# A two-stage FFN kernel: the second stage begins with the batches that the first one finished last

## The chip, the cores and the metric

One core of one Trainium2 chip runs the kernel. The metric is the device time of one execution in microseconds (us); the kernel before took 832.73 us (median of 3 runs, 832.57 to 832.79).

## The reference, cut to what is computed

```python
# x: (32, 128, 2048) f32; one session id, channel count and length for each of the 32 batches
xm  = x * channel_mask
h   = gelu(einsum('bct,bch->bht', xm, W_sess[ids]) + b_sess[ids][:, :, None])   # 128 -> 256
o   = (einsum('bht,hs->bst', h, W2) + b2) * time_mask                           # 256 -> 128
w_q = fp8_e4m3(clip(weight * w_scale))     # w_scale = 448 / max|weight|, weight is 2048 x 2048
x_q = fp8_e5m2(clip(o * x_scale))          # x_scale = 57344 / max|o| over ALL batches
out = x + einsum('bsk,nk->bsn', x_q, w_q) / x_scale / w_scale + bias
```

The scale of `o` needs the maximum over all 32 batches. So the second product can't begin before the first stage is through.

## The kernel before, in words

**Stage one** works in units `u` of 1024 columns, two for each of 32 batches, so u = 0 to 63. Per unit TensorE (PE) multiplies x by the session weight (12 matmuls at L980; x is split into a high and a low part), ScalarE (ACT) applies the gelu, and PE multiplies by W2. The first half of h is always split into a high and a low part (`project0`, 6 matmuls, L995). The second half (`project1`) is either split too, for the units in `SPLIT_H1` (6 matmuls, L1007; ACT writes one more copy at L621 and GpSimd (POOL) subtracts at L541), or is multiplied unsplit in fp32 (L1011; the profile counts 4 matmuls). VectorE (DVE) masks the output (`mask_o`, L765), scans it for its maximum (`scan_o`, L770) and makes the low part of h (`split_h_rest`, L755). SyncE (SP) stores `o` of each batch to `masked_out` in HBM (`store_o`).

**The FFN weight** is scanned for its maximum in 24 parts, one per unit. Then it is rounded to e4m3 in 43 chunks of 768 columns (the last has 512): ACT scales chunk i (`scale_chunk`, L633, which waits until chunk i-2 is rounded), DVE makes its rounding factor (`exponents` L779, `round_at` L784) and POOL adds and subtracts it (`round_chunk`, L535 and L537). `QUANT = SCANS + 2 = 26` says when that begins: POOL rounds chunk i in unit i + QUANT + 1. `EARLY_CHUNKS = 64 - 3 - QUANT = 35` chunks are rounded in stage one, and the 8 "late" ones (35 to 42) after it.

**The seam.** After the last unit DVE reduces the maximum (L844, L848), PE broadcasts it (L1052), DVE makes the scale (L850, L852, L854) and quantizes the first batch of stage two in 5 cuts (L861). PE turns each cut (L1065), ACT writes it back as fp8 (L702), and the products begin (L1071). In between PE runs a few matmuls whose result isn't read (L1047, 8 and then 4).

**Stage two** multiplies the 32 quantized batches by the rounded weight: for each batch 4 products (`n`) of 16 matmuls over 512 output columns, into 4 PSUM banks in turn. The first 16 products are written out as the list `FIRST`: y = 0 to 11 are n = 0, 1, 2 of batches 0 to 3, and y = 12 to 15 are n = 3 of the four. The first three products run side by side. The last quarter of the weight, chunks 32 to 42, is read from y = 12 on only. DVE takes each product out of its bank (`evacuate`, L881, or L901 for n = 3), adding `x + bias`. Product y waits until product y - 4 is out of the bank. Evacuation of n = 0 to 2 waits until POOL has added the bias to that batch's x (`add_bias`, L569, counted by `xb_ready`), and for n = 3 it waits for the small adds of L589 (`x3_ready`).

Each engine works strictly in the order of its program. Behind the seam:

- POOL: bias to x of batch 0 (ahead of the seam), chunks 35, 36, bias of batch 1, chunks 37 to 40, bias of batch 2 (`x2_more[0]`), chunks 41, 42, bias of batch 3 (`x2_more[1]`), four small adds (L589), and then one bias add per batch.
- DVE: 5 cuts, factor of chunk 35, quantization of batch 1, chunks 36 to 38; then, product by product, the evacuation, with the quantization of batches 2, 3 and 4 ahead of y = 2, 5, 10 (`QUANT_AT`) and the factor of a chunk behind y = 4, 5, 6, 7 (`CHUNK_BEHIND`).
- SP: the loads of `o` and x, the transposing DMAs (`turn`, `turn_more`) that lay a quantized batch out for PE, and the stores.

`o` of batches 0 and 1 is read back into `o_in` from unit 40 on, `o` of 2 and 3 after the seam; x of the first batches is read again from HBM.

```python
                dve.wait_ge(y_psum, y + 1 + ONE)          # DVE, product y of batch b
                if n < NC - 1:
                    dve.wait_ge(xb_ready, b + 1)
                    ...
                    evacuate(...)
                pe.wait_ge(y_ready, y + 1)                # PE, ahead of product y (starts at 4)
```

Of the kernel before, what the change touches and what calls it, by code (L numbers as in the profile page):

```python
# [6 lines left out]
def adaln_ffn(nc, x, ids, lens, counts, w_sess, b_sess, w2, b2, weight, bias, out, masked_out, split_w):  # L7
# [33 lines left out]

    SPLIT_H1 = [u for u in range(2, 27)]

# [6 lines left out]
    CHUNKS = -(-WCOLS // CHUNK)  # L50
    QUANT = SCANS + 2

# [12 lines left out]

    QUAD = 4
    FIRST = [(b, n) for b in range(QUAD) for n in range(NC - 1)] + [(b, NC - 1) for b in range(QUAD)]

# [3 lines left out]

    CHUNK_BEHIND = range(4, 12)
    TAIL = [slice(BANK * (NC - 1), BANK * NC - BANK // 2), slice(BANK * NC - BANK // 2, BANK * NC)]
# [8 lines left out]
    with ExitStack() as ctx:  # L83
# [86 lines left out]

        xs = x_sb[:, 1, :]
        q8 = xs[:, 0:T // 2].bitcast(fp8).rearrange("p (r t) -> p r t", r=2)
# [11 lines left out]

        x3 = sb_at("x3", [P, QUAD, BANK], fp32, xh_at)
        x2 = (x_sb[:, 0, :], h1[:, :, :].rearrange("p a n -> p (a n)"))
        x2_more = (sb_at("x2_more0", [P, T], fp32, hh_at)[:, :], sb_at("x2_more1", [P, T], fp32, hl_at)[:, :])
# [122 lines left out]
        def _(sp):  # L310
# [56 lines left out]
            for u in range(UNITS):  # L367
# [37 lines left out]
                if 0 <= i < CHUNKS:  # L405
                    if i >= 3:
                        sp.wait_ge(w_scaled, i - 2)
                    load_chunk(i)
                if u % UPB == 0 and b > 0:
                    sp.wait_ge(o_masked, u)  # L410
                    store_o(b - 1)
                if u == UNITS - 4:

                    sp.wait_ge(xl_ready, UNITS - 2)
                    load_x_again(0, 0, FRONT)
                if u == UNITS // 2:
                    sp.dma_start(bias_sb[:, :], bias.partition_broadcast(P)).then_inc(bias_loaded, 16)
                if u in (UNITS // 2 + 8, UNITS // 2 + 12):
# [24 lines left out]
            turn(1)  # L443
            for r in range(2):
                sp.wait_ge(o_stored[r], 2 * 16)
                load_o(2 + r, r)
            for r in range(2):
                sp.dma_start(x2_more[r][:, FRONT], x[2 + r, :, FRONT]).then_inc(x2_more_loaded[r], 16)
            for b in range(2):

                sp.wait_ge(q_ready, b + 2 + CUTS)
                sp.sem_inc(transpose_turn, 1)
                turn_more(b)
                if b == 1:
                    sp.wait_ge(o_stored[0], 3 * 16)
                    load_o(4, 0)
                    sp.dma_start(x3[:, :, :], x[0:QUAD, :, FRONT.stop:F].rearrange("b c t -> c b t"))\
                      .then_inc(x3_loaded, 16)
                sp.wait_ge(y_ready, (b + 1) * (NC - 1) + FREE4)
                store_y(b, b, FRONT)  # L460
            load_x_again(4, 0)
            sp.wait_ge(o_stored[1], 3 * 16)
            load_o(5, 1)
            load_x_again(5, 1)
            for b in range(2, QUAD):
                sp.wait_ge(y_ready, (b + 1) * (NC - 1) + FREE4)
                store_y(b, b % 2, FRONT)

# [5 lines left out]
            for b in range(QUAD):  # L474
                sp.wait_ge(y_ready, QUAD * (NC - 1) + b + 1 + FREE4)
                sp.dma_start(out[b, :, FRONT.stop:F], x3[:, b, :]).then_inc(y3_stored, 16)

            def step2(i, last):
                for r in range(2):
                    b = i * 2 + r  # L480
                    if not last:
                        sp.wait_ge(q_ready, b + CUTS)
                        load_o(b + 2, r)
                    if not (last and r == 1):
                        sp.wait_ge(y_psum, b * NC + ONE)
                        sp.sem_inc(load_turn, 1)
                        sp.wait_ge(q_ready, b + 1 + CUTS)
                        sp.sem_inc(transpose_turn, 1)
                        turn(1 - r)
                    if last and r == 1:  # L490
                        for n in range(NC - 1):
                            cols = slice(n * BANK, (n + 1) * BANK)
                            sp.wait_ge(y_ready, b * NC + n + 1 + FREE4)
                            sp.dma_start(out[b, :, cols], y_sb[:, r, cols]).then_inc(y_chunk_stored[n], 16)
                        for h, cols in enumerate(TAIL):
                            sp.wait_ge(y_ready, B * NC + h + FREE4)
                            sp.dma_start(out[b, :, cols], y_sb[:, r, cols]).then_inc(y_chunk_stored[NC - 1 + h], 16)
                        continue
                    sp.wait_ge(y_ready, (b + 1) * NC + FREE4)
                    store_y(b, r)  # L500
                    if not last:
                        load_x_again(b + 2, r)


            for r in range(2):
                sp.wait_ge(o_stored[r], 16 * STEPS)
            with sp.Fori(QUAD // 2, STEPS - 1) as i:
# [9 lines left out]
        def _(pool):  # L517
# [54 lines left out]
            pool.wait_ge(bias_loaded, 16)  # L572
            pool.wait_ge(x2_loaded[0], 16)
            add_bias(x2[0], FRONT)
            for i in late[0:2]:
                round_chunk(i)
            pool.wait_ge(x2_loaded[1], 16)
            add_bias(x2[1], FRONT)
            for i in late[2:6]:
                round_chunk(i)  # L580
            pool.wait_ge(x2_more_loaded[0], 16)
            add_bias(x2_more[0], FRONT)
            for i in late[6:]:
                round_chunk(i)
            pool.wait_ge(x2_more_loaded[1], 16)
            add_bias(x2_more[1], FRONT)
            pool.wait_ge(x3_loaded, 16)
            for b in range(QUAD):
                pool.tensor_tensor(x3[:, b, :], x3[:, b, :], bias_sb[:, FRONT.stop:F], ALU.add).then_inc(x3_ready, 1)  # L589
            with pool.Fori(QUAD // 2, STEPS) as i:  # L590
                for r in range(2):

                    pool.wait_ge(x2_loaded[r], i * 16)
                    add_bias(x2[r])

        @block.scalar
        def _(act):
# [77 lines left out]
            for u in range(UNITS):  # L675
# [39 lines left out]
        def _(dve):  # L715
# [94 lines left out]
            for u in range(UNITS):  # L810
                if u == SCANS + 2:
                    weight_scale()
                if u >= 1:
# [3 lines left out]
                    if u == SCANS + 1:  # L817
                        dve.wait_ge(w_scanned, SCANS)
                        dve.wait_ge(floor_ready, 2)
                        dve.tensor_reduce(w_pmax, w_max[:, :], AX.X, ALU.max).then_inc(w_pmax_ready, 1)  # L820
                    scan_o(u - 1, 0, slice(0, UNIT))
                if 0 <= u - QUANT - 1 < EARLY_CHUNKS + 1:
                    exponents(u - QUANT - 1)
                if 0 <= u - QUANT - 1 < EARLY_CHUNKS:
                    round_at(u - QUANT - 1)
                if u + 1 < UNITS:
                    split_h_rest(u + 1)
                if u == 0:
                    dve.tensor_copy(w2h1[:, :], w2_sb[:, 1, :]).then_inc(w2_split, 1)
# [319 lines left out]
```

## Time and profile before

| | before |
|---|---|
| median of 3 runs | 832.73 us |
| the profiled execution's own time | 833.1 us |
| its span, first to last instruction | 831.3 us |
| PE busy | 825.8 us (99%) |
| POOL busy | 511.8 us (62%) |
| DVE busy | 479.5 us (58%) |
| ACT busy | 345.9 us (42%) |
| PE's share of the chain that ended last | 99% |
| HBM read / written | 143.04 / 69.21 MB |

The span is what lies between the first and the last instruction; 1.8 us of the execution's time lie around it. PE is busy nearly all the time and is nearly all of the chain that ends last. So what counts is how many matmuls there are, and where PE stands still.

### The profile page before, as it was taken

To read this page: it belongs to the slowest core of one execution; us is meant where nothing else is said; L and a number is where in the kernel's file an instruction comes from. 1 tells how busy PE (TensorE), PEld (TensorE's weight loads), DVE (VectorE), ACT (ScalarE), POOL (GpSimd) and SP (SyncE) were. 2 spreads that over 40 slices of the span, in tenths; PEclk is the share of its full clock that TensorE was granted. 3 is DMA by queue.
4 is the path that set the end of the run, shared out by engine and by line. 5 is a ranking of instruction groups with operands and counts; after the bars stand their busy time and mean duration, and the time that the engine had idled before them with its cause. 6 is when DMAs were issued, how large, how long until landed. Compare 5 with 4: busy or idle time off the path is not lost.

```text
span 831.3 us, 10181 instructions
## 1 busy us (share of the span) xinstructions
PE 825.8 (99%) x3568; PEld 479.9 (58%) x3568; DVE 479.5 (58%) x499; ACT 345.9 (42%) x372; POOL 511.8 (62%) x238
## 2 busy tenths in 40 slices
PE   9999999999999999999999999999999999999998
PEld 5777777776767676765444444444444444444444
DVE  6989889788888888888553232323232323232322
ACT  7999999988888888973100000000000000000000
POOL 2899999899999999995983242424242423232322
PEclk9999999999999999999999999999999999999999
DMA  7988999877777877657974868686868686868682
GB/s 258 322 321 321 367 339 353 301 285 296 284 289 303 305 267 301 253 187 246 298 295 119 282 214 282 210 285 212 280 213 280 214 283 214 279 213 282 215 248 107
DMA packets 75008, 220.77 MB, mean 266 GB/s; under 512 B 37594, under 2 KB 40930, under 8 KB 55778
## 3 DMA queue, kind: packets, MB, share of 16 engines
q1 hardware_dynamic: 74080, 219.30, 74.5%
q10 hardware_dynamic: 898, 1.09, 0.4%
q8 instruction: 16, 0.26, 0.1%
q14 instruction: 14, 0.11, 0.0%
HBM read 143.04 MB, written 69.21 MB: 255 GB/s over the span
## 4 chain that ended last, share of the span: by engine, by line
PE 99%; issue 0%; POOL 0%; DVE 0%; ACT 0%; POOLq 0%
PE ps_h L1071 53%; PE ps_h L980 22%; PE ps_o L995 11%; PE ps_o L1011 8%; PE ps_o L1007 4%; PE ps_o L934 1%; PE ps_h L1047 0%; PE ps_o L1071 0%; PE ps_o L980 0%; PE ps_o L1065 0%; POOL time L518 0%; PE ps_o L940 0%; PE ps_h L1052 0%; DVE o_and_max L881 0%; ACT x_sb L702 0%
## 5 line engine op out<-in xcount | busy, mean ns | idle before, releaser
L1071 PE MATMUL ps_h<-wqT,x_sb 128*128 128x512 bf16 x1920 | 413.7, 378 | 0.2 <-ACT x_sb L702 0.2
L1071 PEld LDWEIGHTS ps_h<-wqT,x_sb 128*128 128x128 fp8e5 x1920 | 187.7, 98 | 224.4 <-ACT x_sb L702 0.3
L528 POOL TENSOR_TENSOR xl<-x_sb,xh 128x1024 fp32r<-128x1024 f32 x62 | 149.5, 2411 | 16.3 <-ACT xh L607 16.3
L980 PE MATMUL ps_h<-xh,whl 128*128 128x512 f32 x508 | 150.3, 417 | 0.4
L569 POOL TENSOR_TENSOR x_sb<-x_sb,bias_sb 128x2048 f32<-128x2048 f32 (+1 forms) x15 | 66.7, 4447 | 131.7 <-DMA x_sb<-in_x 131.7
L569 POOL TENSOR_TENSOR h<-h,bias_sb 128x2048 f32<-128x2048 f32 (+1 forms) x15 | 66.7, 4443 | 122.7 <-DMA h<-in_x 122.7
L881 DVE SCALAR_TENSOR_TENSOR o_and_max<-ps_h,scales,h 128x512 f32<-128x512 f32 (+1 forms) x59 | 44.0, 746 | 136.2 <-PE ps_h L1071 136.2
L881 DVE SCALAR_TENSOR_TENSOR o_and_max<-ps_h,scales,x_sb 128x512 f32<-128x512 f32 x59 | 44.2, 750 | 133.4 <-PE ps_h L1071 133.4
L980 PEld LDWEIGHTS ps_h<-xh,whl 128*128 128x128 f32 x508 | 94.2, 188 | 42.0 <-issue 21.7
L765 DVE SCALAR_TENSOR_TENSOR o_and_max<-ps_o,b_sb,steps 128x1024 f32<-128x1024 f32 (+1 forms) x65 | 82.2, 1264 | 29.0 <-PE ps_o L1011 27.1
L755 DVE TENSOR_TENSOR hl<-ps_h,hh 128x1024 fp32r<-128x1024 f32 x63 | 76.8, 1219 | 13.4 <-ACT ps_h L614 13.3
L535 POOL TENSOR_TENSOR ws<-ws,wc 128x768 f32<-128x768 f32 (+1 forms) x43 | 72.2, 1679 | 18.2 <-DVE wc L784 16.7
L613 ACT ACTIVATE hh<-ps_h,hbias 128x1024 fp32r<-128x1024 f32 x63 | 70.3, 1115 | 26.7 <-PE ps_h L980 26.7
L980 PE MATMUL ps_h<-xl,whl 128*128 128x512 f32 x254 | 79.1, 392 | 0.0
L770 DVE TENSOR_REDUCE o_max<-o_and_max 128x1 f32<-128x1024 f32 x64 | 77.6, 1212 | 2.2
L537 POOL TENSOR_TENSOR wqT<-ws,wc 128x768 bf16<-128x768 f32 (+1 forms) x43 | 71.8, 1669 | 3.4
L1011 PE MATMUL ps_o<-h,w_sb 128*128 128x512 f32 x156 | 73.4, 592 | 0.0
L622 ACT ACTIVATE h<-ps_h,hbias 128x1024 f32<-128x1024 f32 (+1 forms) x65 | 71.2, 1096 | 0.9 <-PE ps_h L980 0.9
L607 ACT ACTIVATE xh<-x_sb,cmask 128x1024 fp32r<-128x1024 f32 x62 | 71.4, 1151 | 0.4 <-issue 0.4
L614 ACT ACTIVATE ps_h<-ps_h,hbias 128x1024 f32<-128x1024 f32 x63 | 68.0, 1080 | 0.0
L541 POOL TENSOR_TENSOR hl<-h,hh 128x1024 fp32r<-128x1024 f32 x25 | 60.3, 2410 | 10.7 <-ACT h L622 9.8
L980 PEld LDWEIGHTS ps_h<-xl,whl 128*128 128x128 f32 x254 | 47.7, 188 | 11.1
(101 smaller groups left out, 657.2 us busy)
## 6 DMA issues: line engine op xcount, KB each, us to landing
x_sb<-in_x SPq DMA_DIRECT2D x44, 1024.0 KB, 5.7
masked_out<-o_and_max SPq DMA_DIRECT2D x32, 1024.0 KB, 6.8
o_in<-masked_out SPq DMA_DIRECT2D x32, 1024.0 KB, 8.9
out<-o_and_max SPq DMA_DIRECT2D x27, 1024.0 KB, 5.1
wqT<-in_L_ffn_weight SPq DMA_DIRECT2D x23, 684.0 KB, 8.3
wt<-in_L_ffn_weight SPq DMA_DIRECT2D x40, 384.0 KB, 5.5
h<-in_x SPq DMA_DIRECT2D x14, 1024.0 KB, 7.2
whl<-split_w SPq DMA_DIRECT2D x18, 256.0 KB, 6.0
```

Source lines behind the costliest of these rows:

```text
L528: pool.tensor_tensor(xl[:, u % 2, :], x_cols(u), xh[:, u % 2, :].bitcast(fp32), ALU.subtract)\
L535: pool.tensor_tensor(v, v, c, ALU.add).then_inc(w_added, 1)
L537: pool.tensor_tensor(wqT[:, CHUNK_AT[i]], v, c, ALU.subtract).then_inc(w_rounded, 1)
L569: pool.tensor_tensor(to[:, cols], to[:, cols], bias_sb[:, cols], ALU.add).then_inc(xb_ready, 1)
L755: dve.tensor_tensor(hl[:, u % 2, :], h0_of(u), hh[:, u % 2, :].bitcast(fp32), ALU.subtract)\
L765: dve.scalar_tensor_tensor(o_cols(u)[:, cols], ps_o[:, u % 2, cols], b2_sb[:, :], window, ALU.add, ALU.mult)\
L770: dve.tensor_reduce(o_max[:, u + k:u + k + 1], o_cols(u)[:, cols], AX.X, ALU.max, apply_absolute_value=True)\
L881: dve.scalar_tensor_tensor(y_sb[:, r, cols], bank, y_scale, xs[r][:, cols], ALU.mult, ALU.add)\
L980: mm = nc.tensor.matmul(to[:, cols], whl[:, b % SLOTS_W, rows], xs[:, u % 2, cols], start=(k == 0), stop=(k == 2))
L995: nc.tensor.matmul(ps_o[:, u % 2, cols], w[:, :], hs[:, u % 2, cols], start=(k == 0), stop=False)
L1011: mm = nc.tensor.matmul(ps_o[:, u % 2, cols], w2_sb[:, 1, :], h1[:, u % 2, cols], start=False, stop=True)
L1071: mm = nc.tensor.matmul(bank, q[:, k // 2, :, k % 2], wq[:, n, k, cols], start=(k == 0), stop=(k == KT - 1))
```

## The change

Batches are taken in another order in stage two: position p = 0, 1 are batches 30 and 31, and position p >= 2 is batch p - 2. The outputs of batches 30 and 31 still lie in `o_sb`, and are quantized from there. They are neither stored nor loaded. Their x still lies in `x_sb`, and isn't loaded again; the bias is added to it there, and the two small adds for their last 512 columns read it too. The quantized batches move from `x_sb` to the buffer of h1. The weight's rounding begins two units later (QUANT = 28), which leaves 33 early and 10 late chunks (33 to 42), and units 27 and 28 join `SPLIT_H1`. The factor of chunk 33 is made in units 61 and 62, and ACT scales chunk 35 ahead of the seam.

POOL's order becomes: bias to x of position 0, chunk 33, bias of position 1, (wait for the 5 cuts), two small adds, chunks 34 to 39, bias of position 2, chunks 40 to 42, bias of position 3, two small adds. DVE makes chunks 34 to 36 ahead of the evacuations, and chunks 37 to 42 behind y = 2, 4, 5, 6, 7, 8.

```diff
-    SPLIT_H1 = [u for u in range(2, 27)]
+    SPLIT_H1 = [u for u in range(2, 29)]
...
-    QUANT = SCANS + 2
+    QUANT = SCANS + 4
...
-    QUAD = 4
+    QUAD, KEPT = 4, 2
...
-    CHUNK_BEHIND = range(4, 12)
+    CHUNK_BEHIND = (2, 4, 5, 6, 7, 8)
...
-        xs = x_sb[:, 1, :]
+        xs = h1[:, :, :].rearrange("p a n -> p (a n)")
...
-        x2 = (x_sb[:, 0, :], h1[:, :, :].rearrange("p a n -> p (a n)"))
+        x2 = (x_sb[:, 0, :], x_sb[:, 1, :])
...
+        def batch_at(p):
+
+            return B - KEPT + p if p < KEPT else p - KEPT
...
-                if u % UPB == 0 and b > 0:
+                if u % UPB == 0 and 0 < b <= B - KEPT:
                     sp.wait_ge(o_masked, u)
                     store_o(b - 1)
-                if u == UNITS - 4:
-
-                    sp.wait_ge(xl_ready, UNITS - 2)
-                    load_x_again(0, 0, FRONT)
...
+            def load_x_more(r):
+                sp.dma_start(x2_more[r][:, FRONT], x[r, :, FRONT]).then_inc(x2_more_loaded[r], 16)
+
             sp.wait_ge(o_psum, UNITS + 1)
-            load_x_again(1, 1, FRONT)
-            sp.wait_ge(o_masked, UNITS + 1)
-            store_o(B - 1)
+            load_x_more(0)
...
-            for r in range(2):
-                sp.wait_ge(o_stored[r], 2 * 16)
-                load_o(2 + r, r)
-            for r in range(2):
-                sp.dma_start(x2_more[r][:, FRONT], x[2 + r, :, FRONT]).then_inc(x2_more_loaded[r], 16)
+            load_x_more(1)
...
             late = range(EARLY_CHUNKS, CHUNKS)
             pool.wait_ge(bias_loaded, 16)
-            pool.wait_ge(x2_loaded[0], 16)
             add_bias(x2[0], FRONT)
-            for i in late[0:2]:
-                round_chunk(i)
-            pool.wait_ge(x2_loaded[1], 16)
+            round_chunk(late[0])
+            pool.wait_ge(xl_ready, UNITS)
             add_bias(x2[1], FRONT)
-            for i in late[2:6]:
+            pool.wait_ge(q_ready, CUTS)
+            for b in range(KEPT):
+                pool.tensor_tensor(x3[:, b, :], x2[b][:, FRONT.stop:F], bias_sb[:, FRONT.stop:F], ALU.add).then_inc(x3_ready, 1)
+            for i in late[1:7]:
                 round_chunk(i)
             pool.wait_ge(x2_more_loaded[0], 16)
             add_bias(x2_more[0], FRONT)
-            for i in late[6:]:
+            for i in late[7:]:
                 round_chunk(i)
             pool.wait_ge(x2_more_loaded[1], 16)
             add_bias(x2_more[1], FRONT)
             pool.wait_ge(x3_loaded, 16)
-            for b in range(QUAD):
+            for b in range(KEPT, QUAD):
...
+            scale_chunk(EARLY_CHUNKS + 2)
+
             for k in range(CUTS):
...
+                if 0 <= u - QUANT - 1 < EARLY_CHUNKS:
+                    exponents(u - QUANT - 1)
                 if 0 <= u - QUANT - 1 < EARLY_CHUNKS + 1:
-                    exponents(u - QUANT - 1)
-                if 0 <= u - QUANT - 1 < EARLY_CHUNKS:
                     round_at(u - QUANT - 1)
                 if u + 1 < UNITS:
                     split_h_rest(u + 1)
+                if u - QUANT - 1 == EARLY_CHUNKS - 1:
+                    exponents(EARLY_CHUNKS)
...
+            def quantize_kept(r, cols):
                 dve.sem_inc(q_turn, 1)
-                dve.tensor_scalar(to[:, r, cols], o_in[:, r, cols], o_scale, None, ALU.mult, saturate=False)\
+                dve.tensor_scalar(q8[:, r, cols], o_sb[:, r, cols], o_scale, None, ALU.mult, saturate=False)\
                    .then_inc(q_ready, 1)
...
             for k in range(CUTS):
-                quantize(0, 1, k == 0, CUT[k])
+                quantize_kept(0, CUT[k])
 
             late = range(EARLY_CHUNKS, CHUNKS)
-            round_at(late[0])
-            quantize(1, 1, True, slice(0, T))
+            quantize_kept(1, slice(0, T))
...
-                if y in CHUNK_BEHIND and 4 + CHUNK_BEHIND.index(y) < len(late):
+                if y in CHUNK_BEHIND:
                     i = late[4 + CHUNK_BEHIND.index(y)]
```

## Rows read from the trace of the kernel before

**Rows 1.** The page: busy time and shares, and the clock granted to PE in 40 slices.

```profile
PE 825.8 (99%) x3568; PEld 479.9 (58%) x3568; DVE 479.5 (58%) x499; ACT 345.9 (42%) x372; POOL 511.8 (62%) x238
...
PEclk9999999999999999999999999999999999999999
```

**Rows 2.** Timeline of PE (start us, us, what), stage one. Two units apart: split, then unsplit.

```profile
140.79 0.62 PE L1007 MATMUL ps_o<-hh,w2l 128*128 128x512 f32 x2
...
152.17 0.62 PE L1007 MATMUL ps_o<-hh,w2l 128*128 128x512 f32 x2
...
358.46 1.88 PE L1011 MATMUL ps_o<-h,w_sb 128*128 128x512 f32 x4
...
370.24 1.88 PE L1011 MATMUL ps_o<-h,w_sb 128*128 128x512 f32 x4
```

**Rows 3.** Timeline of DVE, from unit 62 to the scale and the first cuts.

```profile
374.73 0.94 DVE L779 TENSOR_SCALAR wE<-ws 128x768 uint16<-128x768 uint16 x1
...
377.08 1.28 DVE L765 SCALAR_TENSOR_TENSOR o_and_max<-ps_o,b_sb,steps 128x1024 f32<-128x1024 f32 x1 [0.19 <-issue]
...
383.92 0.15 DVE L854 TENSOR_SCALAR scales<-scales 128x1 f32<-128x1 f32 x1
384.25 1.80 DVE L861 TENSOR_SCALAR x_sb<-o_in,scales 128x256 fp8e5<-128x256 f32 x5 [0.17 <-DVE scales L854]
```

**Rows 4.** Timeline of POOL around the seam.

```profile
373.84 3.51 POOL L569 TENSOR_TENSOR x_sb<-x_sb,bias_sb 128x1536 f32<-128x1536 f32 x1
386.59 2.61 POOL L535 TENSOR_TENSOR ws<-ws,wc 128x768 f32<-128x768 f32 x1 [9.23 <-DVE wc L784]
```

**Rows 5.** Timeline of DVE, two instructions beside POOL's rows.

```profile
386.43 1.28 DVE L861 TENSOR_SCALAR x_sb<-o_in,scales 128x2048 fp8e5<-128x2048 f32 x1
...
387.81 1.41 DVE L872 TENSOR_TENSOR scales<-scales 128x1 f32<-128x1 f32 x1
```

**Rows 6.** Timeline of POOL behind the seam, up to the last full bias add of batch 3.

```profile
405.97 2.62 POOL L535 TENSOR_TENSOR ws<-ws,wc 128x768 f32<-128x768 f32 x1 [0.81 <-DVE wc L784]
...
410.27 1.64 POOL L535 TENSOR_TENSOR ws<-ws,wc 128x768 f32<-128x768 f32 x1
...
413.59 3.43 POOL L569 TENSOR_TENSOR x_more<-x_more,bias_sb 128x1536 f32<-128x1536 f32 x1
419.38 1.64 POOL L535 TENSOR_TENSOR ws<-ws,wc 128x768 f32<-128x768 f32 x1 [2.37 <-DVE wc L784]
421.10 1.70 POOL L537 TENSOR_TENSOR wqT<-ws,wc 128x768 bf16<-128x768 f32 x1
423.04 1.16 POOL L535 TENSOR_TENSOR ws<-ws,wc 128x512 f32<-128x512 f32 x1 [0.23 <-DVE wc L784]
...
425.38 3.42 POOL L569 TENSOR_TENSOR x_more<-x_more,bias_sb 128x1536 f32<-128x1536 f32 x1
```

**Rows 7.** Timeline of DVE between the evacuations of y = 2 and y = 9.

```profile
400.26 0.74 DVE L881 SCALAR_TENSOR_TENSOR o_and_max<-ps_h,scales,x_sb 128x512 f32<-128x512 f32 x1
...
403.70 0.75 DVE L881 SCALAR_TENSOR_TENSOR o_and_max<-ps_h,scales,h 128x512 f32<-128x512 f32 x1 [2.04 <-PE ps_h L1071]
...
417.11 0.75 DVE L881 SCALAR_TENSOR_TENSOR o_and_max<-ps_h,scales,x_more 128x512 f32<-128x512 f32 x1 [7.76 <-POOL x_more L569]
...
419.22 0.74 DVE L881 SCALAR_TENSOR_TENSOR o_and_max<-ps_h,scales,x_more 128x512 f32<-128x512 f32 x1
...
421.34 1.61 DVE L784 TENSOR_SCALAR wc<-wE 128x512 bf16<-128x512 bf16 x1
...
428.90 0.75 DVE L881 SCALAR_TENSOR_TENSOR o_and_max<-ps_h,scales,x_more 128x512 f32<-128x512 f32 x1 [5.28 <-issue]
```

**Rows 8.** Timeline of PE: the products y = 12, 13, and then 14, 15.

```profile
427.57 7.07 PE L1071 MATMUL ps_h<-wqT,x_sb 128*128 128x512 bf16 x32
434.48 7.07 PE L1071 MATMUL ps_h<-wqT,more 128*128 128x512 bf16 x32
```

**Rows 9.** Timeline of SP's queue: the transposing DMA of batch 4.

```profile
433.00 1.98 SPq L431 DMA_TRANSPOSE x_sb<-x_sb  x1
```

More of the change, by code:

```diff
@@ L454, in _ @@
                 if b == 1:
-                    sp.wait_ge(o_stored[0], 3 * 16)
-                    load_o(4, 0)
-                    sp.dma_start(x3[:, :, :], x[0:QUAD, :, FRONT.stop:F].rearrange("b c t -> c b t"))\
+                    sp.wait_ge(o_stored[0], 2 * 16)
+                    load_o(QUAD - KEPT, 0)
+                    sp.dma_start(x3[:, KEPT:QUAD, :], x[0:QUAD - KEPT, :, FRONT.stop:F].rearrange("b c t -> c b t"))\
                       .then_inc(x3_loaded, 16)
                 sp.wait_ge(y_ready, (b + 1) * (NC - 1) + FREE4)
[L460 to L464, printed above, removed]
+                store_y(batch_at(b), b, FRONT)
+            sp.wait_ge(x3_ready, KEPT)
+            load_x_again(QUAD - KEPT, 0)
+            sp.wait_ge(o_stored[1], 2 * 16)
+            load_o(QUAD + 1 - KEPT, 1)
+            load_x_again(QUAD + 1 - KEPT, 1)
             for b in range(2, QUAD):
                 sp.wait_ge(y_ready, (b + 1) * (NC - 1) + FREE4)
-                store_y(b, b % 2, FRONT)
+                store_y(batch_at(b), b % 2, FRONT)
             sp.wait_ge(y_psum, QUAD * (NC - 1) + 1 + ONE)
@@ L475, in _ @@
                 sp.wait_ge(y_ready, QUAD * (NC - 1) + b + 1 + FREE4)
-                sp.dma_start(out[b, :, FRONT.stop:F], x3[:, b, :]).then_inc(y3_stored, 16)
+                sp.dma_start(out[batch_at(b), :, FRONT.stop:F], x3[:, b, :]).then_inc(y3_stored, 16)
             def step2(i, last):
@@ L482, in step2 @@
                         sp.wait_ge(q_ready, b + CUTS)
-                        load_o(b + 2, r)
+                        load_o(b + 2 - KEPT, r)
                     if not (last and r == 1):
@@ L493, in step2 @@
                             sp.wait_ge(y_ready, b * NC + n + 1 + FREE4)
-                            sp.dma_start(out[b, :, cols], y_sb[:, r, cols]).then_inc(y_chunk_stored[n], 16)
+                            sp.dma_start(out[b - KEPT, :, cols], y_sb[:, r, cols]).then_inc(y_chunk_stored[n], 16)
                         for h, cols in enumerate(TAIL):
                             sp.wait_ge(y_ready, B * NC + h + FREE4)
-                            sp.dma_start(out[b, :, cols], y_sb[:, r, cols]).then_inc(y_chunk_stored[NC - 1 + h], 16)
+                            sp.dma_start(out[b - KEPT, :, cols], y_sb[:, r, cols]).then_inc(y_chunk_stored[NC - 1 + h], 16)
                         continue
                     sp.wait_ge(y_ready, (b + 1) * NC + FREE4)
-                    store_y(b, r)
+                    store_y(b - KEPT, r)
                     if not last:
-                        load_x_again(b + 2, r)
+                        load_x_again(b + 2 - KEPT, r)
             for r in range(2):
-                sp.wait_ge(o_stored[r], 16 * STEPS)
+                sp.wait_ge(o_stored[r], 16 * (STEPS - 1))
             with sp.Fori(QUAD // 2, STEPS - 1) as i:
@@ L591, in _ @@
                 for r in range(2):
-                    pool.wait_ge(x2_loaded[r], i * 16)
+                    pool.wait_ge(x2_loaded[r], i * 16 - 16)
                     add_bias(x2[r])
@@ L705, in _ @@
             for i in range(EARLY_CHUNKS + 2, CHUNKS):
-                scale_chunk(i)
+                if i > EARLY_CHUNKS + 2:
+                    scale_chunk(i)
                 if UNITS - QUANT + 2 <= i + 3 < CHUNKS:
@@ L855, in _, with quantize @@
             dve.wait_ge(scale_step, 5)
-            def quantize(r, loads, first, cols, to=q8):
-                if first:
-                    dve.wait_ge(o_in_loaded[r], loads * 16)
+            def quantize_kept(r, cols):
                 dve.sem_inc(q_turn, 1)
-                dve.tensor_scalar(to[:, r, cols], o_in[:, r, cols], o_scale, None, ALU.mult, saturate=False)\
+                dve.tensor_scalar(q8[:, r, cols], o_sb[:, r, cols], o_scale, None, ALU.mult, saturate=False)\
+                   .then_inc(q_ready, 1)
+            def quantize(r, loads, to=q8):
+                dve.wait_ge(o_in_loaded[r], loads * 16)
+                dve.sem_inc(q_turn, 1)
+                dve.tensor_scalar(to[:, r, :], o_in[:, r, :], o_scale, None, ALU.mult, saturate=False)\
                    .then_inc(q_ready, 1)
             for k in range(CUTS):
-                quantize(0, 1, k == 0, CUT[k])
+                quantize_kept(0, CUT[k])
             late = range(EARLY_CHUNKS, CHUNKS)
-            round_at(late[0])
-            quantize(1, 1, True, slice(0, T))
+            quantize_kept(1, slice(0, T))
             dve.reciprocal(o_inv, o_scale).then_inc(scale_step, 1)
@@ L885, in _ @@
             for r in range(2):
-                dve.wait_ge(o_stored[r], 16 * STEPS)
+                dve.wait_ge(o_stored[r], 16 * (STEPS - 1))
             for y, (b, n) in enumerate(FIRST):
@@ L890, in _ @@
                     k = 2 + QUANT_AT.index(y)
-                    quantize(k % 2, k // 2 + 1, True, slice(0, T), q8_more if k < QUAD else q8)
+                    quantize(k % 2, k // 2, q8_more if k < QUAD else q8)
                 dve.wait_ge(y_psum, y + 1 + ONE)
@@ L912, in step2 @@
                         dve.wait_ge(qT_loaded[1 - r], i * 16 + DMA)
-                        quantize(1 - r, i + 1 + r, True, slice(0, T))
+                        quantize(1 - r, i + r)
                     dve.wait_ge(xb_ready, b + 1)
```

## The prediction

> **What bounds the kernel now.** I read the page first. PE is busy for 99% of the span, at the full granted clock in every slice [rows 1]. Its chain is the one that ends last. So an edit gains only if it takes work from PE or closes a gap of PE, and it costs only if PE waits. I then read the timelines of all engines around the end of stage one and over the first 16 products, because the diff touches nothing else but two units of stage one. The reader is to see three things there: what each step waits for, how far ahead of PE it is, and how much POOL has left. All sums are in the times of the profiled execution (span 831.3 us, its own time 833.1 us). That is 0.37 us above the median of 832.73 us, so I add the changes to the median. This kernel's measurement can tell some 0.2%, or 1.67 us, from no change.
>
> **Units 27 and 28 split.** Two split units lie 152.17 - 140.79 = 11.38 us apart, two unsplit ones 370.24 - 358.46 = 11.78 us [rows 2]. So PE gains 0.20 us per unit, 0.40 us in all. POOL's and ACT's extra work in these two units is what they do in units 2 to 26, and the chunk that POOL had there comes two units later. SP loads the chunks two units later as well. No cost.
>
> **Loads and stores left out.** Two stores and two loads of `o` and most of two loads of x go, some 6 MB. No wait of PE on a DMA stands in the waits, so this gains nothing by itself: 0.
>
> **The seam.** In unit 62 DVE now does `round_at` instead of `exponents`: about 0.5 us instead of 0.94 [rows 3]. But the factor's first half, made a unit earlier, starts the preceding mask 0.1 to 0.2 us late. So the mask of unit 62 could begin 0.3 us before 377.08 [rows 3]. Behind it DVE soon waits for PE's last product instead, so I take 0.1 us as gained (bounds 0 and 0.3). ACT's scaling of chunk 35 needs chunk 33 rounded, which is done at 380.6 by the count that follows, four microseconds ahead of the first cut's turn: 0.
>
> POOL has more to do here. Its bias add of position 0 runs as before from 373.84 [rows 4]. It used to stand idle for 9.23 us after that. Now chunk 33 follows (3.32 us by 413.59 - 410.27 [rows 6]) and the bias of position 1 (3.4). So POOL is busy until 373.84 + 3.4 + 3.32 + 3.4 = 384.0. DVE makes the scale at 383.92 - 0.1 = 383.8 and the first cut at 384.2 [rows 3]. Does POOL's add hold DVE up? The rows show that it can: L872, one element per partition, took 1.41 us from 387.81 and ended at 389.22, just as POOL's 386.59 + 2.61 = 389.20 ended, and POOL's own instruction took 2.61 instead of 1.64 us beside DVE's quantization at 386.43 [rows 4 to 6]. Taken for the scale, that is at most 384.0 - 383.8 = 0.2 us; taken as nothing, 0. I take 0.1, which cancels the gain. The two small adds wait for the cuts and don't touch them. Seam: 0, bounds -0.3 to +0.2.
>
> The Trainium skill (SBUF — State Buffer, "Who interferes with whom") says that a VectorE instruction in a two-port mode or with two SBUF inputs and a GpSimd instruction block each other fully, and that the one issued first wins. The rows of L872 and of the quantization agree. By that rule this change, which fills POOL's idle time with adds, is a risk at the seam: see the third rival.
>
> **Behind the seam: POOL's list grows by a chunk in the wrong place.** From the cuts on, POOL had 8 chunks and 2 big bias adds up to the last one. Now it has 9 chunks, the 2 adds and 2 small ones, but starts with them at 386.1 and finds chunk 34's factor soon. Two places pace it by DVE, and so by PE. I follow it in the old times.
>
> First pace: chunk 38 has its factor made behind y = 4, evacuated at 403.70. Before, chunk 39 had it made in the same place, and POOL took it up at 405.97 after waiting 0.81 [rows 6, 7]. Is POOL there by then? Chunk 37's factor comes behind y = 2, evacuated at 400.26 to 400.9; 1.5 us of DVE brings 401.7 (the evacuation is followed directly by the factor now), and 3.32 us of POOL 405.1. Chunks 34 to 36 are through by 401. So POOL still waits about 0.9 us. From there all is as before, one chunk number lower: the quantization at y = 5 holds the add (2.62 us), the next chunk starts at 410.27, the bias of the third batch ends at 417.0, and y = 6 is evacuated at 417.11 [rows 6, 7].
>
> Second pace: the factor of the next chunk is made behind that evacuation, and POOL takes it up at 419.38. Before, two chunks were left from there, one of them the short one: the last big bias add began at 425.38, ended at 428.80 and let y = 9 go at 428.90 (the row says "issue", but DVE waits for `xb_ready` there, and the times meet). Now three are left. Chunk 40 ends at 419.38 + 3.32 = 422.7. Chunk 41's factor is ready long before (behind the evacuation at 419.22). It ends at 426.0. The short chunk 42 can be scaled by ACT only after chunk 40 is rounded, at 423.5, and its factor waits out both of POOL's instructions of chunk 41, as the one at 421.34 waited (1.61 us) for the one of 421.10 to 422.80 [rows 6, 7]. That is 426.3. It ends with 2.3 us (425.38 - 423.04) at 428.7. Then the bias add of 3.4 ends at 432.1. So y = 9 is evacuated from 432.2 to 432.95 instead of 428.90 to 429.65.
>
> Who waits: PE's product y = 13 needs that bank. It starts one product (6.91 / 2 = 3.45 us) after 427.57, at 431.02 [rows 8]. Before, the bank was free 1.37 us ahead of it. Now it is free 1.9 us too late, 2.0 us with the signal. This time is lost for good, since PE has no idle time to make it up. Later: DVE has the quantization of batch 4 and y = 10, 11 behind the held evacuation, done at about 436.0. SP's queue stores and then issues the transposing DMA of batch 4 at 436.6 instead of 433.00 [rows 9]; by 4.3 us from issue to landing (433.0 to 437.3), or that behind its own 1.98 us, it lands at 440.9 to 442.9. PE needs it at 427.57 + 4 x 3.45 + 2.0 = 443.4. No further stall. The last chunk is rounded at 428.7, and the 16th matmul of y = 12, which reads it, comes at 430.8: free. What a pause of 2 us does to the granted clock no row shows; bounds below 0 aren't possible, above it I allow 1 us in the range, and take 0, the nearest row being the clock that stays full in all slices, the seam's among them [rows 1].
>
> **Sum:** -0.40 + 0 + 0 + 2.0 = +1.6 us: 834.3 us.
>
> **Rivals.**
> 1. *No stall, because what I count as serial overlaps.* It needs 2.0 us out of the count: the 1.0 us by which the add at 405.97 was held (2.62 instead of 1.64), the 0.3 us for which POOL waits for the last factor, and 0.7 us of the 2.37 us that it waits ahead of 419.38 [rows 6]. For it: each is a chance meeting of two instructions, and POOL starts its list behind the seam at once instead of after 386.59. Against: both paces are set by DVE and PE, and they repeat an order that the trace shows. Then only the 0.40 us are left: 832.73 - 0.40 = 832.3 us.
> 2. *Slower: POOL misses the first pace.* Place: chunk 37, between y = 2 and y = 4. POOL has 0.9 us in hand. If one more of its instructions (1.65 us) is held there, everything behind it moves by 0.8 us, one for one: 835.1 us. It decides from 0.9 us of delay on. For it: quantizations and adds do hold each other. Against: in the trace the one ahead of y = 2 was done by 400.3.
> 3. *Slower: POOL's bias add holds the scale at the seam.* It decides once the add of position 1 ends later than 384.1; each microsecond counts in full, up to the whole 3.4. A delay of 0.8 us with the stall of 2.0 us gives 835.1 us. [...] Against: by my sum it ends in time.
>
> **Chances.** The forecast 0.58, with its own range of 833.5 to 835.1; no stall 0.17; the two slower rivals 0.15 and 0.10. A part of the forecast's range lies above 834.4 (832.73 + 1.67), about 0.22 of its 0.58. Faster by over 0.2% would need 1.67 us taken off PE, for which only 0.4 is in sight: 0.02. Slower: 0.22 + 0.14 + 0.07 = 0.43. Within 0.2%: 0.55. The range reaches from no stall to the slower rivals: 832.1 to 835.6 us.
>
> **What would show it.** Right: PE idle for about 2 us ahead of y = 13, released by DVE; DVE's evacuation of y = 9 waiting for POOL until about 46 us behind the first product; 162 matmuls at L1007 (27 units of 6) instead of 150, and no new gap at the seam. Wrong: PE without a gap in the first 60 us of stage two (rival 1), POOL's chunk 38 taken up without a wait (rival 2), or the gap ahead of L1065 grown beyond 0.5 us with a long L854 or first cut (rival 3). A PE clock below full after the gap would add to it.

## The result, and the profile after

The changed kernel took 834.55 us (median of 15 runs, 833.97 to 835.36), beside 832.97 us for the kernel before (15 runs, 832.28 to 833.22). The ratio is 1.002, with a 95% interval of 1.0012 to 1.0028. So it is 1.58 us slower, just inside what I had called no change (0.2%, 1.67 us), though the interval is clear of 1.

| | before | after |
|---|---|---|
| median | 832.97 us | 834.55 us |
| the profiled execution's own time | 833.1 us | 834.0 us |
| its span | 831.3 us | 832.2 us |
| PE busy | 825.8 us | 824.6 us |
| POOL busy | 511.8 us | 516.5 us |
| HBM read / written | 143.04 / 69.21 MB | 138.85 / 67.11 MB |

The profiled execution of after is the lowest of its 15 runs, 0.58 us below the median, and that of before lies 0.13 us above its own. So the two spans differ by 0.9 us only, and 0.88 + 0.58 + 0.13 = 1.59 us brings the two accounts together. The sums below are made within the traces.

The page of the changed kernel, as in [rows 1], and the group of the products, with the idle time ahead of them and what ended it:

```profile
PE 824.6 (99%) x3572; PEld 480.6 (58%) x3572; DVE 477.6 (57%) x499; ACT 348.3 (42%) x374; POOL 516.5 (62%) x240
...
PEclk9999999999999999999999999999999999999999
...
L1078 PE MATMUL ps_h<-wqT,h 128*128 128x512 bf16 x1920 | 413.8, 378 | 2.1 <-DVE o_and_max L888 1.9
```

The products (now L1078) have one new releaser: a DVE evacuation, 1.9 us, once. The timeline of PE shows where. First the kernel before at the seam, then the changed kernel; its last three rows answer to [rows 8]:

```profile
384.70 0.58 PE L1065 MATMUL ps_o<-ident,x_sb 128*128 128x128 fp8e5 x4 [0.48 <-issue]
385.45 1.47 PE L1071 MATMUL ps_h<-wqT,x_sb 128*128 128x512 bf16 x6 [0.17 <-ACT x_sb L702]
```

```profile
383.50 0.58 PE L1072 MATMUL ps_o<-ident,h 128*128 128x128 fp8e5 x4 [0.45 <-issue]
384.25 1.47 PE L1078 MATMUL ps_h<-wqT,h 128*128 128x512 bf16 x6 [0.17 <-ACT h L703]
...
426.37 3.62 PE L1078 MATMUL ps_h<-wqT,h 128*128 128x512 bf16 x16
431.90 3.61 PE L1078 MATMUL ps_h<-wqT,h 128*128 128x512 bf16 x16 [1.92 <-DVE o_and_max L888]
435.35 7.07 PE L1078 MATMUL ps_h<-wqT,more 128*128 128x512 bf16 x32
```

The reader is to see that the first product starts at 384.25 (before at 385.45, so 1.20 us earlier), that y = 12 starts at 426.37 (before 427.57, still 1.20 us earlier), and that y = 13 then starts 5.53 us later instead of 3.45. So PE loses 2.08 us there, of which 1.92 us stand as idle time. -1.20 + 2.08 = +0.88 us is the difference of the spans. y = 14, 15 and batch 4 follow without a gap. The clock stayed full through the pause and behind it (busy time of PE and granted clock in two stretches of 2 us):

```profile
430.00:432.00 2.00, 0.10 (x1) 1.00 0.00 0
432.00:434.00 2.00, 2.00 (x10) 1.00 0.00 0
```

DVE and POOL of the changed kernel, the rows that answer to [rows 6, 7]:

```profile
400.26 1.64 POOL L533 TENSOR_TENSOR ws<-ws,wc 128x768 f32<-128x768 f32 x1 [0.69 <-DVE wc L786]
...
404.77 2.62 POOL L533 TENSOR_TENSOR ws<-ws,wc 128x768 f32<-128x768 f32 x1 [1.14 <-DVE wc L786]
...
412.38 3.43 POOL L567 TENSOR_TENSOR x_more<-x_more,bias_sb 128x1536 f32<-128x1536 f32 x1
418.18 1.64 POOL L533 TENSOR_TENSOR ws<-ws,wc 128x768 f32<-128x768 f32 x1 [2.37 <-DVE wc L786]
...
427.50 3.42 POOL L567 TENSOR_TENSOR x_more<-x_more,bias_sb 128x1536 f32<-128x1536 f32 x1
```

```profile
415.90 0.75 DVE L888 SCALAR_TENSOR_TENSOR o_and_max<-ps_h,scales,x_more 128x512 f32<-128x512 f32 x1 [7.76 <-POOL x_more L567]
...
431.01 0.75 DVE L888 SCALAR_TENSOR_TENSOR o_and_max<-ps_h,scales,x_more 128x512 f32<-128x512 f32 x1 [5.93 <-POOL x_more L567]
```

POOL's last big bias add begins at 427.50 and ends at 430.92. DVE, which had waited 5.93 us for it, evacuates y = 9 at 431.01 and is done at 431.76, and PE starts y = 13 at 431.90. In the kernel before, the same three were 425.38, 428.90 and, with time in hand, 431.02.

At the seam PE waits no longer than before. Its idle time ahead of the first turn is 0.45 us (0.48 before), and DVE's scale takes 0.15 us as in [rows 3]:

```profile
379.46 3.44 POOL L567 TENSOR_TENSOR x_sb<-x_sb,bias_sb 128x1536 f32<-128x1536 f32 x1
```

```profile
382.74 0.15 DVE L858 TENSOR_SCALAR scales<-scales 128x1 f32<-128x1 f32 x1
383.04 3.00 DVE L863 TENSOR_SCALAR h<-o_and_max,scales 128x256 fp8e5<-128x256 f32 x6
```

PE reaches the seam 1.20 us earlier than in the kernel before, for three reasons. This is PE's last matmul pair of `project0` (L995 before, L1002 after) in units 0, 27 and 30 and in two neighbours later on, in both kernels:

```profile
13.17 0.73 PE L995 MATMUL ps_o<-hl,w2h 128*128 128x512 f32 x2
...
167.98 0.63 PE L995 MATMUL ps_o<-hl,w2h 128*128 128x512 f32 x2
...
185.65 0.63 PE L995 MATMUL ps_o<-hl,w2h 128*128 128x512 f32 x2
...
321.11 0.63 PE L995 MATMUL ps_o<-hl,w2h 128*128 128x512 f32 x2
...
327.17 0.63 PE L995 MATMUL ps_o<-hl,w2h 128*128 128x512 f32 x2
```

```profile
12.50 0.74 PE L1002 MATMUL ps_o<-hl,w2h 128*128 128x512 f32 x2
...
167.29 0.63 PE L1002 MATMUL ps_o<-hl,w2h 128*128 128x512 f32 x2
...
184.61 0.63 PE L1002 MATMUL ps_o<-hl,w2h 128*128 128x512 f32 x2
...
320.06 0.63 PE L1002 MATMUL ps_o<-hl,w2h 128*128 128x512 f32 x2
...
325.96 0.63 PE L1002 MATMUL ps_o<-hl,w2h 128*128 128x512 f32 x2
```

The changed kernel's execution is 0.67 us ahead in its first unit already, where the program is the same: the start differs from run to run. It is 0.69 us ahead in unit 27, before the first newly split half, and 1.04 us in unit 30, so the two units gave 0.35 us. Another 0.16 us are one unit of the kernel before that took 6.06 us (321.11 to 327.17) where the changed kernel took 5.90; why isn't known. So without the different start the traces give 2.08 - 0.35 - 0.16 = +1.57 us, which fits the +1.58 of the medians.

### The profile page after: what moved, and what is told of

It is laid out like the page before. It is cut to its first block, busy times and chain, and to the rows that moved or that the text cites. A ratio compares the mean times of both kernels' runs of the same rounds, so it can differ in the third digit from the quotient of the medians.

```text
span 832.2 us, 10173 instructions
## 1 busy us (share of the span) xinstructions
PE 824.6 (99%) x3572; PEld 480.6 (58%) x3572; DVE 477.6 (57%) x499; ACT 348.3 (42%) x374; POOL 516.5 (62%) x240
## 3 DMA queue, kind: packets, MB, share of 16 engines
HBM read 138.85 MB, written 67.11 MB: 247 GB/s over the span
## 4 chain that ended last, share of the span: by engine, by line
PE 96%; POOL 2%; DVE 1%; issue 1%; ACT 0%; POOLq 0%; DVEq 0%
PE ps_h L1078 50%; PE ps_h L987 22%; PE ps_o L1002 11%; PE ps_o L1018 8%; PE ps_o L1014 4%; POOL ws L533 1%; POOL x_more L567 1%; PE ps_o L941 1%; POOL wqT L535 1%; DVE wE L781 0%; DVE wc L786 0%; PE ps_h L1054 0%; PE ps_o L1078 0%; DVE o_and_max L888 0%; PE ps_o L987 0%
## 5 line engine op out<-in xcount | busy, mean ns | idle before, releaser
L1078 PE MATMUL ps_h<-wqT,h 128*128 128x512 bf16 x1920 | 413.8, 378 | 2.1 <-DVE o_and_max L888 1.9
L1078 PEld LDWEIGHTS ps_h<-wqT,h 128*128 128x128 fp8e5 x1920 | 187.6, 98 | 226.6 <-issue 2.4
L567 POOL TENSOR_TENSOR x_sb<-x_sb,bias_sb 128x2048 f32<-128x2048 f32 (+1 forms) x30 | 133.3, 4444 | 255.9 <-DMA x_sb<-in_x 255.9
L888 DVE SCALAR_TENSOR_TENSOR o_and_max<-ps_h,scales,x_sb 128x512 f32<-128x512 f32 x118 | 88.2, 748 | 270.5 <-PE ps_h L1078 270.4
L539 POOL TENSOR_TENSOR hl<-h,hh 128x1024 fp32r<-128x1024 f32 x27 | 65.0, 2409 | 12.9 <-ACT h L621 12.1
L1018 PE MATMUL ps_o<-h,w_sb 128*128 128x512 f32 x148 | 69.7, 592 | 0.0
L632 ACT ACTIVATE ws<-wt,scales 128x768 f32<-128x768 f32 (+1 forms) x43 | 40.0, 931 | 27.0 <-POOL wqT L535 27.0
L781 DVE TENSOR_SCALAR wE<-ws 128x768 uint16<-128x768 uint16 (+1 forms) x43 | 40.7, 947 | 4.4 <-ACT ws L632 4.3
```

The lines of the kernel that those rows point to most:

```text
L567: pool.tensor_tensor(to[:, cols], to[:, cols], bias_sb[:, cols], ALU.add).then_inc(xb_ready, 1)
L888: dve.scalar_tensor_tensor(y_sb[:, r, cols], bank, y_scale, xs[r][:, cols], ALU.mult, ALU.add)\
L1018: mm = nc.tensor.matmul(ps_o[:, u % 2, cols], w2_sb[:, 1, :], h1[:, u % 2, cols], start=False, stop=True)
L1078: mm = nc.tensor.matmul(bank, q[:, k // 2, :, k % 2], wq[:, n, k, cols], start=(k == 0), stop=(k == KT - 1))
```

## The experiments

My theory was that POOL's list, with one more full chunk between the bias adds of positions 2 and 3, holds the evacuation of y = 9, and through its bank PE. The rivals were that the kept batches, the other order of batches or the loads cause the gap, and that the seam costs something.

**e1: the bias of position 3 ahead of chunks 40 to 42.**

```diff
-            for i in late[7:]:
-                round_chunk(i)
             pool.wait_ge(x2_more_loaded[1], 16)
             add_bias(x2_more[1], FRONT)
+            for i in late[7:]:
+                round_chunk(i)
```

> The changed kernel with one edit: POOL adds the bias of position 3 ahead of chunks 40 to 42 instead of behind them. My theory (POOL's list makes y = 9 late): that add fits into POOL's idle time ahead of chunk 40 (2.4 us) nearly whole, y = 9 is let go in time, the gap of PE ahead of y = 13 goes, and the last chunk ends some 1 us later than in the changed kernel, still ahead of y = 12's last matmul. So about 2.0 us less than the changed kernel: 832.5 us, 0.4 to 0.5 below the kernel before. Rival (the kept batches, the other order of batches or the loads make the gap): the gap stays at about 2 us whatever POOL's order is, 834.5 us. Rival (the last quarter of the weight becomes the bound): y = 9 is in time, but PE waits within y = 12 for the last chunk, up to 1.5 us.

Measured: 832.34 us (11 runs), beside 833.07 us for the kernel before (21 runs); ratio 0.9991, interval 0.9982 to 1.0. Timeline of PE and of POOL:

```profile
426.95 7.07 PE L1078 MATMUL ps_h<-wqT,h 128*128 128x512 bf16 x32
```

```profile
412.97 6.83 POOL L567 TENSOR_TENSOR x_more<-x_more,bias_sb 128x1536 f32<-128x1536 f32 x2
419.76 1.64 POOL L533 TENSOR_TENSOR ws<-ws,wc 128x768 f32<-128x768 f32 x1
...
426.73 1.16 POOL L533 TENSOR_TENSOR ws<-ws,wc 128x512 f32<-128x512 f32 x1 [0.23 <-DVE wc L786]
427.96 2.02 POOL L535 TENSOR_TENSOR wqT<-ws,wc 128x512 bf16<-128x512 f32 x1
```

y = 12 and y = 13 are one piece of 32 matmuls again, with no gap. Both bias adds run back to back, and the second fills POOL's idle time: chunk 40 starts 6.79 us behind the beginning of the first add, only 1.0 us later than in the changed kernel (418.18 - 412.38 = 5.80). The order alone takes away the whole loss: 2.2 us by the two medians, which weren't taken side by side; against the kernel before in the same runs, the changed kernel was 1.58 us above and e1 is 0.73 us below. The last chunk ends at 427.96 + 2.02 = 429.98; the 16th matmul of y = 12 starts at 426.95 + 15 x 0.216 = 430.19. So 0.2 us are left there. I had not foreseen that DVE's quantization for y = 10 would hold POOL's last instruction (2.02 us instead of 1.15).

**e4: the kept batches alone** (the old QUANT and the old split units).

```diff
-    SPLIT_H1 = [u for u in range(2, 29)]
+    SPLIT_H1 = [u for u in range(2, 27)]
-    QUANT = SCANS + 4
+    QUANT = SCANS + 2
-    CHUNK_BEHIND = (2, 4, 5, 6, 7, 8)
+    CHUNK_BEHIND = (2, 4, 5, 6)
```

> Only the batches kept on chip: QUANT = SCANS + 2 and SPLIT_H1 = 2 to 26 as before, 8 late chunks, their factors behind y = 2, 4, 5, 6. My theory: the kept batches and the bias ahead of the seam cost nothing and gain nothing; POOL has only the short chunk 42 between the bias adds of positions 2 and 3, so y = 9 goes some 3 us ahead of need and PE has no gap: the time of the kernel before, 832.9 us, within 0.2. Rival (leaving 6 MB of transfers out gains by itself): below 832.5. Rival (the seam's adds or the order of batches cost something): above 833.3.

Measured: 832.97 us (11 runs) beside 833.07; ratio 0.9997, interval 0.9988 to 1.0006. No gap of PE in the products. POOL's last big add:

```profile
420.84 3.43 POOL L567 TENSOR_TENSOR x_more<-x_more,bias_sb 128x1536 f32<-128x1536 f32 x1
```

It begins at 420.84 and is done 3.4 us later, at 424.3, some 4.5 us ahead of the kernel before. DVE has y = 9 out of its bank at 425.1, and PE starts y = 13 at 427.45 + 3.45 = 430.9. So this bank has 5.8 us in hand, not the 3 us that I had expected. And leaving 6 MB out, the other order of batches and the adds ahead of the seam neither gain nor cost more than the interval, some 0.1%.

**e2: one add of chunk 41 cut short.**

```diff
-                pool.tensor_tensor(v, v, c, ALU.add).then_inc(w_added, 1)
+                n = 64 if i == 41 else chunk_cols(i)
+                pool.tensor_tensor(v[:, 0:n], v[:, 0:n], c[:, 0:n], ALU.add).then_inc(w_added, 1)
```

> The changed kernel, but POOL's add for chunk 41 covers 64 of its 768 columns, so the rest of that chunk isn't rounded. The add of 1.64 us becomes some 0.2 to 0.3. My theory: POOL ends 1.4 us earlier, but the short chunk's factor waits for ACT and DVE, so 1.0 to 1.4 us of it come through: PE's gap ahead of y = 13 falls from 1.9 to 0.5 to 0.9 us. Rival (the gap isn't POOL's): it stays at 1.9 us.

Measured: 833.28 us in one run. The other 704 columns of the chunk don't get their add, so that part of the weight is left unrounded and the output is off. The run serves for its trace alone.

```profile
421.74 0.30 POOL L534 TENSOR_TENSOR ws<-ws,wc 128x64 f32<-128x64 f32 x1
...
424.45 1.15 POOL L534 TENSOR_TENSOR ws<-ws,wc 128x512 f32<-128x512 f32 x1 [0.69 <-DVE wc L787]
...
426.79 3.43 POOL L568 TENSOR_TENSOR x_more<-x_more,bias_sb 128x1536 f32<-128x1536 f32 x1
```

```profile
426.60 3.62 PE L1079 MATMUL ps_h<-wqT,h 128*128 128x512 bf16 x16
431.21 3.61 PE L1079 MATMUL ps_h<-wqT,h 128*128 128x512 bf16 x16 [1.00 <-DVE o_and_max L889]
```

The gap is 1.00 us instead of 1.92. The add took 0.30 us, 1.34 us less, but 0.69 us were spent waiting for the short chunk's factor instead of 0.23, so 0.9 us came through. That is just outside the 0.5 to 0.9 us that I had written. The gap follows POOL's work, and DVE's and ACT's part of the last chunk limits how far.

**e6: two extra adds in the kernel before.**

```diff
             pool.wait_ge(x2_more_loaded[1], 16)
+            pool.tensor_tensor(raw[:, 0:2, :], raw[:, 0:2, :], raw[:, 0:2, :], ALU.add)
+            pool.tensor_tensor(raw[:, 2:4, :], raw[:, 2:4, :], raw[:, 2:4, :], ALU.add)
             add_bias(x2_more[1], FRONT)
```

> The kernel BEFORE with two extra adds of 512 columns on POOL (results not used) ahead of the last big bias add: 2 x 1.03 = 2.06 us. My theory: the bank of y = 9 had 1.37 us in hand there, so PE gets a gap ahead of y = 13 of 2.06 - 1.37 = 0.7 us (0.5 to 0.9 idle). So the kernel before has the same weak place, and the change only used up what it had in hand. Rival (the gap needs the kept batches or the new order): no gap.

Measured: 833.93 us in one run, beside 832.88 us for the kernel before (15 runs).

```profile
425.44 1.04 POOL L586 TENSOR_TENSOR raw<-raw 128x512 f32<-128x512 f32 x1
...
427.44 3.43 POOL L569 TENSOR_TENSOR x_more<-x_more,bias_sb 128x1536 f32<-128x1536 f32 x1
```

```profile
427.61 3.62 PE L1073 MATMUL ps_h<-wqT,x_sb 128*128 128x512 bf16 x16
431.86 3.61 PE L1073 MATMUL ps_h<-wqT,x_sb 128*128 128x512 bf16 x16 [0.63 <-DVE o_and_max L883]
```

The two adds put the bias add off by 427.44 - 425.44 = 2.00 us, and the gap is 0.63 us. So the kernel before has the same weak place with 1.4 us in hand, and nothing else of the change is needed to open it.

**e3: the bias add laid across the scale and the first cut.**

```diff
             pool.wait_ge(xl_ready, UNITS)
+            pool.tensor_tensor(raw[:, 0:2, :], raw[:, 0:2, :], raw[:, 0:2, :], ALU.add)
             add_bias(x2[1], FRONT)
```

> The changed kernel with an extra add of 512 columns on POOL (some 1.2 us, its result isn't used) ahead of the bias of position 1, so that this bias add ends about 1.2 us later and lies across DVE's scale and first cut. By the third rival of the prediction POOL's add holds DVE: the cut starts only when the add ends, about 1.0 us later, and the gap of PE ahead of the first L1072 grows from 0.45 to about 1.4 us. If DVE isn't held, the seam stays as it is. L858, one element per partition, tells whether so small an instruction is held too: 0.15 us if not, about 1 us if so.

Measured: 835.02 us in one run (all lines are one or two numbers higher than in the changed kernel). POOL's add, DVE's scale and cuts, and PE's first turn:

```profile
380.84 3.42 POOL L567 TENSOR_TENSOR x_sb<-x_sb,bias_sb 128x1536 f32<-128x1536 f32 x1
```

```profile
383.12 0.15 DVE L859 TENSOR_SCALAR scales<-scales 128x1 f32<-128x1 f32 x1
383.42 3.64 DVE L864 TENSOR_SCALAR h<-o_and_max,scales 128x256 fp8e5<-128x256 f32 x6
```

```profile
384.51 0.58 PE L1073 MATMUL ps_o<-ident,h 128*128 128x128 fp8e5 x4 [1.09 <-issue]
```

The add runs from 380.84 to 384.26. The scale, one element per partition, falls into it and takes 0.15 us: it isn't held. The cut that is due at 383.42 is held: the six instructions of that row take 3.64 us instead of 3.00, and PE's gap is 1.09 us instead of 0.45. The first of the six, by itself, took 0.99 us, and 0.35 us in the changed kernel; it ended at 384.41, 0.15 us behind the add. I had expected a gap of some 1.4 us: the add ended 0.84 us after the cut was due, not 1.0, and 0.64 us of that came through. So rival 3 of the prediction is half right. POOL's add does hold DVE at the seam, but it holds the cut and not the scale, and not one for one. In the changed kernel the add ended at 382.9, 0.14 us ahead of the cut at 383.04.

**e5: POOL delayed by another 1.5 us.**

```diff
             pool.wait_ge(x2_more_loaded[1], 16)
+            pool.tensor_tensor(raw[:, 0:3, :], raw[:, 0:3, :], raw[:, 0:3, :], ALU.add)
             add_bias(x2_more[1], FRONT)
```

> The changed kernel with one more add of 768 columns on POOL (result not used) right ahead of the bias of position 3; by the 1.03 us that 512 columns took in e3_late_seam_bias, 1.5 us. My theory: PE's idle time ahead of y = 13 grows one for one from 1.9 to 3.4 us, the granted clock stays full, and the transposing DMA of batch 4, issued 1.5 us later too, still lands in time for the next batch: 1.5 us more than the changed kernel. Rival (a pause that long costs more than itself): matmuls longer than 379 ns behind it, or a clock below 1, or a second gap ahead of y = 16.

Measured: 837.91 us in one run, 3.4 us more than the changed kernel. The theory's own part holds: the add took 1.47 us and the gap is 3.36 us. The rival holds too. Timeline of PE, and the busy time of PE with the granted clock (PEclk) in stretches of 2 us:

```profile
427.17 3.62 PE L1079 MATMUL ps_h<-wqT,h 128*128 128x512 bf16 x16
434.15 5.30 PE L1079 MATMUL ps_h<-wqT,h 128*128 128x512 bf16 x16 [3.36 <-DVE o_and_max L889]
439.29 1.03 PE L1079 MATMUL ps_h<-wqT,more 128*128 128x512 bf16 x4
```

```profile
434.00:436.00 2.00, 1.85 (x5) 0.55 0.00 0
436.00:438.00 2.00, 2.00 (x8) 0.60 0.21 86
438.00:440.00 2.00, 2.00 (x11) 1.00 0.95 327
```

Behind the pause the clock was 0.55 and then 0.60 of full. These are means of stretches that mix two levels: from 435 to 437 us it reads 0.50, which is the lower of the two (1.2 instead of 2.4 GHz), and from 437.6 us on it is full again. y = 13 took 439.29 - 434.15 = 5.14 us instead of 3.45: 1.69 us on top of the pause. y = 16 still followed without a gap, with its transposing DMA issued at 437.36.

**e7: one step further than e1.**

```diff
-    SPLIT_H1 = [u for u in range(2, 29)]
+    SPLIT_H1 = [u for u in range(2, 30)]
-    QUANT = SCANS + 4
+    QUANT = SCANS + 5
-    CHUNK_BEHIND = (2, 4, 5, 6, 7, 8)
+    CHUNK_BEHIND = (1, 2, 3, 4, 6, 7, 8)
...
-            for i in late[1:7]:
+            for i in late[1:8]:
```

> e1_bias_first taken one step further: QUANT = SCANS + 5, unit 29 split too, 11 late chunks, chunk factors behind y = 1, 2, 3, 4, 6, 7, 8, seven chunks ahead of the bias of position 2. The extra split gives 0.2 us. In e1_bias_first the last chunk was done some 0.2 us ahead of the last matmul of y = 12, and POOL's remaining waits (0.7 and 1.1 us) don't hold a whole chunk (3.3 us). My theory: PE waits 0.5 to 1.5 us for the last chunks within y = 12, so 832.6 to 833.6 us, 0.3 to 1.3 above e1_bias_first. Rival (POOL's waits absorb the chunk): 832.1 us, better than e1_bias_first.

Measured: 833.18 us (11 runs) beside 832.88 us for the kernel before (15 runs); ratio 1.0006, interval 0.9997 to 1.0015.

```profile
425.81 3.40 PE L1078 MATMUL ps_h<-wqT,h 128*128 128x512 bf16 x15
430.45 3.84 PE L1078 MATMUL ps_h<-wqT,h 128*128 128x512 bf16 x17 [1.24 <-POOL wqT L535]
```

PE stops within y = 12, ahead of its last matmul, for 1.24 us, released by POOL's rounding of the last chunk. The extra split unit can't pay for that. Of the schedules that were run e1 is the best, and it is 0.7 us below the kernel before by the medians (832.34 against 833.07), with an interval that just reaches 1.0.

## Why the prediction was right

The forecast was 834.3 us against 832.73, so +1.6; measured were +1.58. The mechanism and the size of its main term are right. That the total comes within 0.1 us is in part luck: the two terms measure 2.08 - 0.35 = +1.73 in the traces, and 0.16 us that no term foresaw bring it down. Step by step:

- **Bound.** PE's idle time decides, as forecast. The only new idle time of PE in the products is the one ahead of y = 13.
- **Units 27 and 28.** Forecast -0.40 us; the trace shows -0.35.
- **Loads and stores.** Forecast 0; e4 shows no effect beyond some 0.1%.
- **The seam.** Forecast 0 (-0.3 to +0.2); PE's gap went from 0.48 to 0.45 us. The reason that I gave for a possible +0.2, that POOL's add holds the scale itself, was wrong. I had it from L872, which is a `tensor_tensor`; e3 shows that a `tensor_scalar` of one element per partition isn't held and the cut is. The changed kernel's add ended 0.14 us ahead of the first cut, so that the seam cost nothing was a near thing.
- **First pace.** Forecast: POOL takes up chunk 37 at 401.7 and waits 0.9 us ahead of chunk 38. Shifted by the 1.20 us, that is 400.5; measured were 400.26 and a wait of 1.14 us. The held add took 2.62 us as forecast. The take-up time came out by luck. By the rows it was to be 400.9 + 1.5 = 402.4, not the 401.7 that I wrote, which leaves out the evacuation itself; and DVE was 1.1 us earlier at y = 2 than I had assumed (its evacuation began at 398.00, where 400.26 - 1.20 = 399.06 was due). The two slips cancel nearly. They don't touch the time, since POOL waits for chunk 38's factor in either case.
- **Second pace.** Forecast for the evacuation of y = 9: 432.2, shifted 431.0; measured 431.01.
- **Who waits.** Forecast 2.0 us; measured 2.08.
- **Afterwards.** Forecast for the transposing DMA of batch 4: 436.6, shifted 435.4, with no further gap; measured 435.10, no gap:

```profile
435.10 1.98 SPq L432 DMA_TRANSPOSE h<-h  x1
```

- **The clock.** I took 0 for a pause of 2 us with up to 1 us in the range. In the changed kernel it is 0. In e5 a pause 1.4 us longer cost another 1.7 us by the clock, so the allowance was too small for a stall a little longer, and my range would have missed it. That the pause of the changed kernel stayed short enough was not worked out ahead: no row of the kernel before could tell.

The Trainium skill (SBUF — State Buffer, "Who interferes with whom") has VectorE in a two-port mode and GpSimd block each other, and whichever was issued first goes on. Both cases stand in the traces: the cut in e3, issued behind POOL's add, took 0.99 us instead of 0.35, and POOL's add of 404.77, issued behind DVE's quantization, took 2.62 us instead of 1.64. The section lists `tensor_scalar` only as an operation that can enter such a mode; the scale, a `tensor_scalar` of one element per partition, took 0.15 us beside the add.

What is left open: the two medians that give e1 its 2.2 us against the changed kernel weren't taken in the same runs. Why the start differs by 0.7 us from one execution to another was not looked into. e2, e3, e5 and e6 are one run each, so they are read by their traces and not by their times. Where between a pause of 1.94 and one of 3.36 us the clock begins to fall was not tried. And of the changed kernel's 15 runs only the fastest was traced; whether the 0.14 us at the seam hold in the others isn't shown.

## What to carry to other kernels

Where each engine works through a list in order, put each entry by the time at which somebody waits for it: the bias add that held a PSUM bank stood behind three chunks that nobody needed yet. Ahead of adding work to a list, work out for every consumer behind it how much it has in hand (here 1.4 us), since a gain of 0.2 us per unit isn't worth a full entry of 3.3 us that goes past such a place. A short stall of PE may cost only itself (1.92 us here), a longer one the clock as well (3.36 us).

## What the runs showed of the hardware

- A pause of PE of 1.92 us left the granted clock full, and so did one of 1.94 us in e3. One of 3.36 us (e5, one run) was followed by a lower clock (0.55 and 0.60 in two stretches of 2 us), which cost 1.69 us more.
- Beside a running add of POOL, DVE's `tensor_scalar` of 128x1 took 0.15 us, its usual time, while one of 128x256, due 0.84 us ahead of the add's end, took 0.99 us instead of 0.35 and ended 0.15 us behind the add (e3).
- A quantization of DVE that was issued first held POOL's add in turn: 2.62 us instead of 1.64 (changed kernel, 404.77), and 2.02 instead of 1.15 us in e1.
